# Opening of a six-sublayer kernel: weights staged in pieces in order of use, in memory of later weights

## The reference

```python
x = x + 0.5 * _L0_ffn_ref(_layernorm(x), w12, w3, shared_w1, shared_w2, shared_w3, router_w, expert_bias)
x = x + _L0_attn_ref(_layernorm(x), ...)      # gated linear attention
x = x + 0.5 * _L0_ffn_ref(_layernorm(x), ...)
x = x + 0.5 * _L1_ffn_ref(_layernorm(x), W1, b1, W2, b2)   # W1, W2 quantized to -1, 0, 1
x = x + _L1_attn_ref(_layernorm(x), ...)      # window attention
x = x + 0.5 * _L1_ffn_ref(_layernorm(x), ...)
```

```python
shared = silu(xf @ shared_w1.T) * (xf @ shared_w2.T) @ shared_w3.T
scores = sigmoid(xf @ router_w.T)
_, top_idx = top_k(scores + expert_bias, 2)
```

## Time and profile before

| What | us or share |
|---|---|
| median of three runs | 1905.88 |
| profiled execution, first to last instruction | 1904.6 |
| PE busy | 1700.2 (89%) |
| DVE busy | 1164.4 (61%) |
| ACT busy | 857.4 (45%) |
| POOL busy | 591.3 (31%) |
| first up product of the first sequence starts | 42.10 |

### The profile page before, as it was taken

How to read it: one execution, slowest core, us unless ns; L and a number is a source line. 1 busy time by engine, 2 the same in 40 slices (tenths; PEclk the granted TensorE clock), 3 DMA queues, 4 the chain that set the end, 5 groups by cost and what they waited for, 6 DMA issues and landing times. The chain is left out here.

```text
span 1904.6 us, 42712 instructions
## 1 busy us (share of the span) xinstructions
PE 1700.2 (89%) x15082; PEld 1117.5 (59%) x15083; DVE 1164.4 (61%) x2413; ACT 857.4 (45%) x1479; POOL 591.3 (31%) x549
## 2 busy tenths in 40 slices
PE   1999989999879999998999989999688889899898
PEld 0556556666546666665556556665355657677466
DVE  5766775555446555555565555555576567576676
ACT  3444443333255554554333324343355455554664
POOL 0333230000334544213323210001687444343332
PEclk9999999999989999999999999999799999999999
DMA  7321122333221111001101023332223022121001
GB/s 268 86 77 62 62 93 85 98 99 98 52 34 23 22 33 28 6 1 40 43 31 43 24 89 100 99 99 72 55 51 55 0 69 69 36 69 36 12 33 45
DMA packets 98053, 114.31 MB, mean 60 GB/s; under 512 B 10736, under 2 KB 88592, under 8 KB 97296
## 3 DMA queue, kind: packets, MB, share of 16 engines
q1 hardware_dynamic: 79504, 79.02, 14.1%
q0 software_dynamic: 18432, 33.64, 7.2%
HBM read 64.26 MB, written 48.35 MB: 59 GB/s over the span
## 5 line engine op out<-in xcount | busy, mean ns | idle before, releaser
L1619 PE MATMUL ps<-xt_hi,wsh 128*128 128x512 f16 x512 | 195.3, 381 | 17.4 <-DVE aqkv_lo L1043 13.2
L1620 PE MATMUL ps<-xt_lo,wsh 128*128 128x512 f16 x512 | 195.2, 381 | 0.0
L1621 PE MATMUL ps<-xt_hi,wsh 128*128 128x512 f16 x512 | 195.0, 381 | 0.0
L1619 PE MATMUL ps<-later_hi,work 128*128 x576 | 187.8, 326 | 1.9
L1621 PE MATMUL ps<-later_hi,work 128*128 x576 | 187.6, 326 | 0.0
L1620 PE MATMUL ps<-later_lo,work 128*128 x576 | 187.6, 326 | 0.0
L809 ACT ACTIVATE work<-ps 128x512 f32<-128x512 f32 x128 | 76.4, 597 | 198.3 <-PE ps L1621 198.0
L614 POOL DMA_INDIRECT later_hi<-expert_y,gather_rows x64 | 89.2, 1394 | 232.9 <-issue 227.7
L614 POOL DMA_INDIRECT yg<-expert_y,gather_rows x64 | 81.4, 1272 | 245.2 <-issue 224.2
L1619 PE MATMUL ps<-wsh,work 128*128 128x256 f16 x512 | 141.9, 277 | 16.5 <-DVE work L1202 10.1
L1364 DVE SCALAR_TENSOR_TENSOR work<-ps,work 128x256 f32<-128x256 f32 x144 | 69.7, 484 | 131.1 <-ACT work L851 131.1
(11 more groups left out here) (261 smaller groups left out, 4378.4 us busy)
## 6 DMA issues: line engine op xcount, KB each, us to landing
work<-expert_x SPq DMA_DIRECT2D x144, 128.5 KB, 2.1
expert_y<-work SPq DMA_DIRECT2D x144, 128.0 KB, 1.9
yg<-in_w_later SPq DMA_DIRECT2D x16, 510.0 KB, 3.6
expert_x<-work SPq DMA_DIRECT2D x32, 128.5 KB, 3.5
values<-wsh SPq DMA_DIRECT2D x8, 512.0 KB, 3.2
later_hi<-values SPq DMA_DIRECT2D x16, 256.0 KB, 4.8
later_lo<-values SPq DMA_DIRECT2D x16, 256.0 KB, 4.7
out_x<-x SPq DMA_DIRECT2D x8, 512.0 KB, 2.9
```

Of the source, the lines that this page charges most:

```text
L1619: nc.tensor.matmul(out_, a[0], b[0], start=start, stop=False)
L1620: nc.tensor.matmul(out_, a[0], b[1], start=False, stop=False)
L1621: return nc.tensor.matmul(out_, a[1], b[0], start=False, stop=stop)
```

## The change

**Staging memory.** The staging buffers leave `work`. Eight buffers of 1024 float32 lie in the upper part of the memory of the later weights (`later_hi`, `later_lo`), behind the place of its seventh chunk. `staging_left` is gone.

**Order of loads.** The first sequence of `x` comes before `consts`. The weights come in pieces of 1024 (or 768) columns: the router, the first and second halves of `w_sh1` and `w_sh2` by hidden columns, then `w_sh3` in two. Then the second sequence of `x`, `rows` and `cols`, the ternary weights in four pieces, the other six sequences of `x`, `g_o` and `a_qkv`. PE waits for the pieces it needs, at q = 0, q = 4 and the first `down`. POOL's scaling and clearing is waited for by none of the opening's steps any more.

**Moved into the first two sequences.** The sums of absolute values come at k = 6, k = 7 and the end of the first sequence, the matmul, the thresholds, the comparisons and the splitting of `g_o` and `a_qkv` in the second. The first comparison goes from DVE to POOL.

```diff
-        stage = Carve()([NST, CH])
+        STAGE_AT = 7 * LCH
+        stage = [later[n // 4][:, STAGE_AT + n % 4 * 2 * PIECE:STAGE_AT + (n % 4 + 1) * 2 * PIECE].bitcast(F32) for n in range(NST)]
...
         @block.sync
-            for m, (name, n) in enumerate(loads):
...
+            for k in range(OPENING):
+                sp.dma_start(staged_piece(k), source_of(k)).then_inc(staged[slot_of(k)], 16)
+            sp.dma_start(x[:, TPS:2 * TPS, :], xd[:, TPS:2 * TPS, :]).then_inc(x_loaded[1], 16)
...
+            for j in range(4):
+                if j:
+                    sp.wait_ge(w_lo_done, TERN_SLOT[j] + 1)
...
+            sp.dma_start(x[:, 2 * TPS:, :], xd[:, 2 * TPS:, :]).then_inc(x_loaded[2], 16)
+            for k in range(OPENING, len(PIECES)):
+                sp.wait_ge(w_lo_done, slot_of(k) + 1)
...
                 if not earlier(n):
-                    staging_left(sp)
                     for c in range(NSEQ * LPS):
...
         POOL, body
+                    if is_second(g) and not earlier(n):
+                        pool.wait_ge(tern, 8)
+                        for j in range(4):
+                            dst, w = ternary_part(j)
+                            ternary_loaded(pool, j)
+                            nc.gpsimd.tensor_scalar(dst, w, thr[:, j // 2, 1:2], None, ALU.is_lt).then_inc(tern_low, 1)
                     dispatch(g + 1, 1 - u)
...
         ACT, body
+                        if is_second(g) and not earlier(n) and k in (0, 1, 3):
+                            halves_hi(OPENING + (0, 1, 3).index(k))
...
         DVE, routing(k)
+                            if not earlier(n) and k >= 6:
+                                ternary_sum(k - 6)
                         elif is_second(g):
+                            if not earlier(n) and k in (0, 1, 3):
+                                halves_lo(OPENING + (0, 1, 3).index(k))
+                            if not earlier(n) and k == 3:
+                                ternary_bounds()
+                            if not earlier(n) and k >= 4:
+                                ternary_signs(k - 4)
...
                     take(1)
+                    if is_first(g) and not earlier(n):
+                        ternary_sum(2)
+                        ternary_sum(3)
...
         PE
-            pe.wait_ge(tern, 2)
-            nc.tensor.matmul(ps[:, 7, 0:2], const("ones"), tsum[:], start=True, stop=True).then_inc(tern_sum, 1)
-            pe.wait_ge(w_lo_done, FIRST)
+            pe.wait_ge(w_lo_done, 1)
```

More of the change, by code:

```diff
@@ L271, in load_of, with columns_of @@
[L271 to L282, removed]
+        PIECE = 1024
+        HALF = HSH // 2
+        AQ = KT * 3 * D // 2
+        def columns_of(w, half):
+            return tuple(a.rearrange("p (k h) -> p k h", k=KT)[:, :, half * HALF:(half + 1) * HALF] for a in w)
@@ new lines, in part_of @@
+        def part_of(w, at, n):
+            return tuple(a[:, None, at:at + n] for a in w)
+        PIECES = [("w_r", part_of(wr, 0, KT * NE)),
+                  ("w_sh1", columns_of(wsh1, 0)), ("w_sh2", columns_of(wsh2, 0)),
+                  ("w_sh1", columns_of(wsh1, 1)), ("w_sh2", columns_of(wsh2, 1)),
+                  ("w_sh3", part_of(wsh3, 0, PIECE)), ("w_sh3", part_of(wsh3, PIECE, PIECE)),
+                  ("g_o", part_of(go, 0, PIECE)), ("a_qkv", part_of(aqkv, 0, AQ)), ("a_qkv", part_of(aqkv, AQ, AQ))]
@@ new lines, in build, with slot_of, staged_piece, piece_loaded @@
+        stage = [later[n // 4][:, STAGE_AT + n % 4 * 2 * PIECE:STAGE_AT + (n % 4 + 1) * 2 * PIECE].bitcast(F32) for n in range(NST)]
+        assert STAGE_AT % 2 == 0 and STAGE_AT + 8 * PIECE <= LCH * NSEQ * LPS
+        def slot_of(k):
+            return k if k < OPENING else k - 4
+        def staged_piece(k):
+            own = PIECES[k][1][0]
+            return stage[slot_of(k)][:, 0:own.shape[1] * own.shape[2]].rearrange("p (k n) -> p k n", k=own.shape[1])
+        def piece_loaded(eng, k):
+            eng.wait_ge(staged[slot_of(k)], 16 if k < OPENING else 32)
@@ L773, in _, with halves_hi @@
         def _(act):
[L774 to L780, removed]
+            def halves_hi(k):
+                name, dst = PIECES[k]
+                piece_loaded(act, k)
+                nc.scalar.activation(dst[0], staged_piece(k), ACT.Copy, scale=rms_col if name == "g_o" else WS).then_inc(w_hi_done, 1)
             def later_hi(c):
@@ L1038, in _, with halves_lo @@
         def _(dve):
[L1039 to L1045, removed]
+            def halves_lo(k):
+                name, dst = PIECES[k]
+                dve.wait_ge(w_hi_done, k + 1)
+                nc.vector.scalar_tensor_tensor(out=dst[1], in0=staged_piece(k), scalar=rms_col if name == "g_o" else WS, in1=dst[0],
+                                               op0=ALU.mult, op1=ALU.subtract).then_inc(w_lo_done, 1)
             def later_lo(c):
@@ L1684, in down @@
                         pe.wait_ge(s["y_taken"], (g + G0) * 2 + half + 1)
+                        if is_first(g) and not earlier(n):
+                            pe.wait_ge(w_lo_done, OPENING)
+                        if is_second(g) and not earlier(n) and half == 1:
+                            pe.wait_ge(tern, 8)
                         for t in range(2 * half, 2 * half + 2):
@@ L1697, in body @@
                     for q in range(SU):
+                        if is_first(g) and not earlier(n) and q % 4 == 0:
+                            pe.wait_ge(w_lo_done, 3 if q == 0 else 5)
                         up(q)
+                        if is_second(g) and not earlier(n) and q == 2:
+                            pe.wait_ge(tern, 4)
+                            for half in range(2):
+                                ins = nc.tensor.matmul(ps[:, 7, 0:2], const("ones"), tsum[:, half], start=half == 0, stop=half == 1)
+                            ins.then_inc(tern_sum, 1)
                         if is_first(g):
@@ L1790, in ffn0 @@
                 if not earlier(n):
-                    staging_left(pe)
                     pe.wait_ge(halves_set, 2)
```

120 lines of the change are left out of this document (64 added, 56 removed).

## The result

The changed kernel took **1912.22 us** (median of 5 runs, 1910.67 to 1912.67), the kernel before 1905.88 beside it (5 runs, 1902.55 to 1913.01). The ratio is 1.0034, with an interval of 1.0017 to 1.0050: slower by 0.3%, where 1904.4 was forecast. The profiled execution of the changed kernel spans 1910.3 us against 1904.6, so the difference of 5.7 in the two traces is that of the medians, 6.3, within their spread.

The account below looks back on a forecast made before the run. PE was taken to set the time, with its large idle times in the opening. Up(4) earlier, slow clock and loss over two sequences, -10.5 + 2.7 + 6.3 = -1.5 us, took 1905.9 to 1904.4 us, range 1895 to 1912.

Parts of the forecast that it names:

- ACT takes chunk 0 at k = 1: Opening: ACT's wait for chunk 0 of the later weights, until 42.5, holds up silu(2), product(2) and up(4).
- The gain at up(4): First sequence: up(4) starts at 45.1 instead of 55.57, 10.5 us earlier.
- the slow clock there: At up(4): 13 matmuls run slow behind some 18 us of PE idling, 2.7 us lost.
- Rival 1: Opening's DMA queue: zero writes and chunk 0 go at 357 GB/s, chunk 0 2.9 us earlier; 1899.2 us, chance 0.13.
- rival 2: Opening: PE's early start counts in full, 28 us off and 6.3 back; 1884 us, chance 0.04.
- Loss over the two sequences: 6.3 us: First two sequences: moved work and waits for POOL's comparisons delay PE by 6.3 us, bounds 2.9 and 10.
- The sum: Whole kernel: -10.5 + 2.7 + 6.3 = -1.5 us, giving 1904.4 us.
- everything but POOL: Second sequence, on the old clock: everything except POOL's queue was taken 2.9 us later.
- POOL's next scatter needs rows that DVE places: Second sequence: DVE places these rows behind its last low half, so POOL's comparisons don't delay the scatter.
- The comparison: Second sequence: each 128x1024 threshold comparison on POOL takes 1.90 us, bounds 1.2 and 3.5.
- Rival 3: Second sequence: POOL and DVE block each other, up to 3 us more lost; 1907.4 us, chance 0.18.
- Rival 4: Second sequence: POOL's comparison is dear; 6.3 us each for 9.5 us slower, 1918.3 us at 7; chance 0.09.

Follow-up runs that it names:

- experiment 2: Changed kernel, with chunk 0 of the later weights taken only at the first sequence's end, others one place later, four in the seventh: 1903.1 us, ratio 0.9986.
- experiment 1: Changed kernel, with the four comparisons that went to POOL on DVE again, each ahead of its ternary step: 1913.35 us, ratio 1.0034.
- Experiment 6: Changed kernel, with all ternary work (comparisons on DVE) and the splitting of g_o and a_qkv at k = 1 of the first sequence: 1899.6 us, ratio 0.9968.
- experiment 4: Changed kernel, POOL still comparing, with DVE's four ternary steps behind its last step of the second sequence: 1907.84 us, ratio 1.0013.
- experiment 7: Experiment 1 with one chunk at the first sequence's end, three in each of sequences 2 to 6, none in the seventh: 1886.83 us, ratio 0.9903.
- experiment 8: Changed kernel, with 20 extra 512-column matmuls on PE ahead of up(7) of the second sequence: 1913.17 us, ratio 1.0036.
- experiment 3: Changed kernel with the edits of experiments 1 and 2 together: 1899.67 us, ratio 0.9974.
- experiment 5: Changed kernel, with 60 extra 512-column matmuls on PE behind up(3) of the first sequence: 1906.34 us, ratio 1.0009.

## Why the prediction was wrong

**What held.** The step "ACT takes chunk 0 at k = 1" gave 42.5 for chunk 0 and 45.1 for up(4); they came at 42.41 and 44.87. The gain at up(4) was 10.7 for 10.5, the slow clock there 2.69 for 2.7. up(0) came at 16.80 and not near 14. The pieces that it needs were split by 11.9, and the router's matmuls ran from 14.11; but up(0) also waits for the semaphore that says that its PSUM banks are free (L1172, `DVEq` in the row of 16.80), and that stands in DVE's queue behind the low halves of all seven opening pieces, those for `down` too. The prediction had left this wait out; the stall hid the 3 us. Rival 1 (a faster queue) and rival 2 (the early start counts in full) are out as the change stands; experiment 2 shows that PE runs on from up(3) without a stall once ACT's queue is freed of chunk 0, which is the start of rival 2's gain.

**What failed: "Loss over the two sequences: 6.3 us".** By the first up product of the last sequence it measured 7.4 + 7.2 = 14.6 (more idle time, and further slow stretches), above its upper bound of 10.

1. *The clock was charged once.* The sum took 2.7 us for the slow start behind the long stall, and none for the new waits further on, though the earlier trace rows showed 0.60 us matmuls behind a wait of only 2.56. The wait ahead of the first sequence's last low half was as forecast (2.37, for 1.25 + 1.2), and the slow stretch behind it was not in the sum. The three further slow stretches cost 7.2 us. Without them the step comes to 7.4, within its bounds, and the sum to 1905.9 - 10.7 + 2.7 + 7.4 = 1905.3.
2. *POOL's queue was moved forward in full.* The walk left "everything but POOL" later and took POOL 7.8 us earlier with up(4). But its scatters depend on rows that DVE places behind PE's last `down` of the first sequence, which had become 2.37 us of waiting and 2.51 of slow matmuls later. POOL was ready to compare 2.9 us earlier, not 7.8. The prediction used just this dependence for the second sequence ("POOL's next scatter needs rows that DVE places"), and not for the first.
3. *The comparison was mis-sized:* 2.85 us where 1.90 was taken, within the bounds of 1.2 and 3.5. Points 2 and 3 explain the first ternary step: forecast at 102.3 - 7.8 = 94.5, it started at 100.35, later by 4.9 + 0.95.
4. *Rival 3 was real, as a part.* Beside POOL's comparisons the ternary step took 2.15 and 2.13 us, and 1.28 once POOL was idle; the routing product took 1.22, against 0.42 for its equals. That is (2.15 + 2.13 - 2 x 1.28) + (1.22 - 0.42) = 2.5 us on DVE, where up to 3 was put. Rival 3 by its own number, 1907.4, would still have been short by the clock. The Trainium skill, "SBUF — State Buffer", Who interferes with whom, has a DVE instruction with two SBUF inputs contend with a GpSimd instruction that reads SBUF; the trace agrees in part. Behind the start of each of the last three comparisons one such step was 0.80 to 0.87 us longer; others that ran beside them took their usual time (the low half of a product, 0.67 at 103.03; a routing step, 0.42 at 105.89; the low half of a chunk, 1.22 at 107.94), and none was held up for a whole comparison, as the lock that the prediction cites would have it.

Rival 4 (a comparison of over 6.3 us) didn't happen; the dearest took 3.28.

In the second sequence the points work on each other: a wait makes PE slow, slow PE makes DVE's placing late, late placing makes POOL late, and POOL makes the next wait. That is read from the timelines; only the last link was tested alone, by experiment 1. Experiment 6 takes the added work out of this circle and gets the waits of the kernel before. How the gain divides between idle time and clock is read from the traces (7.4 and 7.2 us lost in the changed kernel's, 0.6 and none in experiment 6's, up to 160 us); between POOL's lateness, its price and the contention it was not separated. Experiments 1 and 4 remove parts, and each found other waits of 2.6 to 3.7 us in their place.

## What to carry to other kernels

Work moved into an engine's idle time is not free because the sum of idle time is larger: ask which step stands behind it in the queue, on every engine in the circle, and whether that engine's own start has moved with the rest. Charge each new wait of TensorE of some 2 us twice, as the wait and as a possible slow stretch behind it: in the changed kernel waits of 1.82 to 5.06 us were followed by stretches that lost 2.3 to 2.5 us each, while behind 2.01 there, and behind 3.04 in experiment 4, nothing was lost. And where a prefetch is taken in the middle of a queue, look first at when its data can come: taking chunk 0 only behind the first sequence brought 19.2 us by the last sequence, and 9.1 at the end, until the chunks crowded in the seventh sequence were spread too (experiment 7).

## What the runs showed of the hardware

- **A wait of the same length did not always bring the clock down.** The wait of 2.37 us ahead of the last `down` of the first sequence was followed by 0.42 us matmuls in the changed kernel and in experiment 1, by the usual 0.27 in experiments 4 and 8; in experiments 2, 3, 5 and 7 the same wait was followed by a slow stretch only 1.2 to 2.0 us later (1.55 to 1.66 us lost). At the same place, the kernel before waited 1.25 us and stayed fast. One profiled execution is thus one draw, and a slow stretch is a risk with a price, not a fixed cost. The runs can't say what decides it.
- **The column of the granted clock missed the first slow stretch of an execution and marked the others.** It says 1.00 over the slow start of up(0) in the kernel before, whose matmuls start 0.425 us apart (1.2 GHz), and over that of the changed kernel (16.80 to 19.31). Over the four stretches of the table it says 0.50 or 0.51. It also says 0.50 in the changed kernel from 38.10 to 43.20, where PE ran nothing. At the start of an execution the spacing of the matmuls is the surer sign. The mean over the execution fell from 0.980 to 0.969.

First a window of the kernel before, then three of the changed one, columns as in the earlier trace rows:

```profile
42.10:47.40 5.30, 5.30 (x13) 1.94 (x14) 1.81 (x9) 1.46 (x2) 1.53 (x3) 1.00 0.74 179
```
```profile
16.80:19.30 2.50, 2.50 (x6) 0.84 (x7) 2.47 (x5) 2.46 (x5) 1.44 (x2) 1.00 1.03 400
44.87:50.40 5.53, 5.53 (x14) 1.90 (x15) 4.52 (x10) 0.81 (x3) 0.00 (x0) 0.50 0.32 99
64.50:71.00 6.50, 6.46 (x52) 4.80 (x53) 3.02 (x11) 2.42 (x3) 3.89 (x4) 0.50 0.24 84
```

- **POOL's comparison held up one two-input step of DVE, not all.** Beside the comparisons a `scalar_tensor_tensor` of 128x1024 took 2.15 and 2.13 us (1.28 alone) and one routing product 1.22 (0.42 alone), while the two-input steps of 0.67, 0.42 and 1.22 us beside the same comparisons were not longer than elsewhere. Experiments 2, 5 and 8, with the same order of steps, show the same lengths; in experiment 4, with another order, other steps were the long ones (a low half took 1.31 for 0.68).
- **A comparison with a threshold from memory is slow on POOL.** 128x1024, float32 to half precision, took 2.83 to 3.28 us, and DVE did it in 0.75 (experiment 6's timeline, the row below), a factor of 3.8 or more. The Trainium skill, "GPSIMD Engine Reference", 4.1 Engine selection, calls one-input elementwise work "roughly line-rate" there; for this form the measurement says otherwise.

```profile
33.22 0.75 DVE L1102 TENSOR_SCALAR w1q<-later_lo,thr 128x1024 f16<-128x1024 f32 x1
```
